# Six layers over sixteen images on one core: due values for each stage and layer in place of one for each stage

## The reference, cut to what matters

```python
x = L0(x, ctx, mask)   # cross attention with masked context, output projection, residual, layer norm
x = L1(x, ctx, ctx)    # cross attention, projection, residual, layer norm
# L2 has three parts:
x = x + causal_self_attention(ln1(x)) @ m_proj_w + m_proj_b     # "SELF"
x = x + cross_attention(ln2(x), ctx) @ c_proj_w + c_proj_b      # "CROSS"
x = x + relu(ln3(x) @ f_w1 + f_b1) @ f_w2 + f_b2                # "FFN", hidden width 1024
x = L3(x, ctx)         # layer norm, cross attention with weights rounded to {-1, 0, 1} * mean|W|
```

## Time and profile before

| | |
|---|---|
| median of 3 runs | 1466.26 us (1465.84 to 1468.56) |
| the profiled execution | 1464.82 us |
| its span, first to last instruction | 1463.1 us |
| instructions | 42292 |
| busy share: PE, DVE, ACT, POOL | 96%, 69%, 54%, 33% |
| mean granted TensorE clock | 0.991 |

### The profile page before, as it was taken

How to read it: one execution, slowest core, us unless ns; L and a number is a source line. 1 busy time by engine, 2 the same in 40 slices (tenths; PEclk the granted TensorE clock), 3 DMA queues, 4 the chain that set the end, 5 groups by cost and what they waited for, 6 DMA issues and landing times.

```text
span 1463.1 us, 42292 instructions
## 1 busy us (share of the span) xinstructions
PE 1404.4 (96%) x18408; PEld 1138.3 (78%) x18408; DVE 1005.1 (69%) x1895; ACT 783.9 (54%) x1305; POOL 481.4 (33%) x511
## 2 busy tenths in 40 slices
PE   4999999999999999999999999999989999899998
PEld 3777777777777777777777777778989999677775
DVE  3667677698787776666666677778686666656664
ACT  2565655655656555555555666665423334565663
POOL 6122213344444453332332221112485555000100
PEclk8999999999999999999999999999999999999999
DMA  7101000100000000000000100000000000000000
GB/s 290 37 26 43 23 26 15 52 9 16 9 9 9 31 16 2 2 2 2 2 2 16 45 9 9 15 9 23 30 1 1 2 1 8 16 30 30 30 24 30
DMA packets 14000, 34.79 MB, mean 24 GB/s; under 512 B 2167, under 2 KB 7543, under 8 KB 12407
## 3 DMA queue, kind: packets, MB, share of 16 engines
q1 hardware_dynamic: 13815, 32.09, 6.7%
HBM read 27.89 MB, written 4.19 MB: 22 GB/s over the span
## 4 chain that ended last, share of the span: by engine, by line
PE 82%; DVE 8%; ACT 5%; issue 2%; DMA 1%; POOL 1%; SPq 0%; DVEq 0%; ACTq 0%; POOLq 0%
PE ps L549 10%; PE ps L718 9%; PE ps L655 7%; PE ps L682 7%; PE ps L600 6%; PE ps L731 5%; PE ps L699 5%; PE ps L572 5%; PE ps L744 5%; PE ps L560 5%; ACT s_PU L841 4%; DVE s_nm L966 4%; PE ps L660 2%; PE ps L679 2%; PE ps L539 2%
## 5 line engine op out<-in xcount | busy, mean ns | idle before, releaser
L966 DVE TENSOR_REDUCE s_nm<-ps 128x8 fp32r<-128x960 f32 (+1 forms) x352 | 395.2, 1168 | 132.8 <-PE ps L600 74.8
L841 ACT ACTIVATE s_PU<-ps 120x1024 f32<-120x1024 f32 (+1 forms) x288 | 273.1, 1028 | 161.2 <-PE ps L660 161.2
L1105 POOL TENSOR_TENSOR s_xs<-s_xs,s_rowv 128x512 f32<-128x512 f32 x96 | 126.4, 1317 | 508.8 <-DVE s_nt L909 460.9
L655 PE MATMUL ps<-s_Qs,s_KH 32*120 32x256 f32 (+2 forms) x4608 | 180.3, 286 | 5.9 <-DVE s_xs L987 2.8
L655 PEld LDWEIGHTS ps<-s_Qs,s_KH 32*120 32x120 f32 (+1 forms) x4608 | 150.3, 181 | 41.2 <-issue 31.2
L549 PE MATMUL ps<-s_xT,s_W 128*128 128x256 f32 x640 | 163.4, 399 | 10.6 <-DMA s_xT<-x_t 9.4
L850 ACT ACTIVATE s_Os<-ps 128x512 f32<-128x512 f32 x160 | 94.4, 596 | 128.5 <-PE ps L682 83.4
L718 PE MATMUL ps<-s_W,s_oT 128*128 128x256 f32 x640 | 156.6, 387 | 1.3 <-ACT s_oT L857 0.9
L794 ACT ACTIVATE s_Qs<-ps,s_colv 128x256 fp32r<-128x256 f32 x160 | 67.2, 472 | 148.5 <-PE ps L549 148.5
L549 PEld LDWEIGHTS ps<-s_xT,s_W 128*128 128x128 f32 x640 | 118.2, 195 | 35.9 <-issue 11.1
L682 PE MATMUL ps<-s_PU,s_Vp 120*32 120x256 f32 x2048 | 126.3, 383 | 6.8 <-DVE s_nm L966 5.5
(11 more groups left out here) (89 smaller groups left out, 2334.6 us busy)
## 6 DMA issues: line engine op xcount, KB each, us to landing
s_cT<-ctx_t SPq DMA_DIRECT2D x32, 240.0 KB, 2.6
s_W<-w_att SPq DMA_DIRECT2D x5, 1024.0 KB, 5.0
s_xs<-x_nat SPq DMA_DIRECT2D x4, 1024.0 KB, 11.8
s_xT<-x_t SPq DMA_DIRECT2D x16, 256.0 KB, 2.7
out<-s_xs SPq DMA_DIRECT2D x16, 256.0 KB, 2.0
s_rowv<-rows SPq DMA_DIRECT2D x6, 512.0 KB, 4.2
s_W<-w_ff SPq DMA_DIRECT2D x2, 1024.0 KB, 5.1
s_mi<-mask SPq DMA_DIRECT2D x8, 120.0 KB, 3.7
```

The lines of the kernel that those rows point to most:

```text
L655: e.matmul(banks[j][0:n, wide * x:wide * x + wide], kz[row[j], lk, g, c, k0:k0 + n], q[row[j], lq, g, qs_], start=(x == 0 and y_ == 0), st ...
L841: t = e.activation(P_of(i, k)[0:n, :, :], pair("B", i, k)[0:n, :, :], ACT.Exp, scale=0.25)
L966: e.tensor_reduce(o, v, AX.X, ALU.max, negate=True).then_inc(sem["max"])
L1105: e.tensor_tensor(xs[:, b, :, :], xs[:, b, :, :], row2(layer, 0), ALU.add).then_inc(sem["pool"])
```

## The change

Only tables change. `WANT` has, for 40 of its names, six numbers in place of one, in the order L0, L1, SELF, CROSS, FFN, L3 (0 where the layer has no such stage), and a new function `want_of` picks the number of the image's layer. Other names keep a single number, mostly a new one. `STAY` goes from 0.121 to 0.656. The stages, their instructions, durations, buffers and the due values of the loads are the same.

```diff
-WANT = dict(xT=-3, cT=-4, mi=-4, bo=-0.9, N=0.88, T=-0.79, Te=-1.18, Q=0.15, Qh=3.01, Ql=-0.26, K=-0.32, Kh=1.79, Kl=0.17,
-            K0=1.54, V=0.81, Ve=3.52, mf=-1.83, A=0.45, max=0.53, M=0.88, mTe=1.15, B=1.08, exp=1.59, cap=2.76, PV=1.76,
-            PVe=2.77, ON=2.29, ONe=2.21, OT=3.16, OTe=1.33, O=-0.25, y=4.16, st=4.05, rs=2.36, ln=0.56, lng=3.08, X=1.12,
-            F1=-0.17, Fa=-0.09, Fv=-1.71, Hl=0.99, F2=2.13, out=2.2)
+WANT = dict(xT=-3, cT=-4, mi=-4, bo=(-1.68, 0.22, -6.66, -2.81, 8.53, -0.8), N=(0, 0, 8.9, 13.27, 16, 15.87),
+            T=(0, 0.35, -0.56, -0.63, -0.63, -1.54), Te=(0, -3.63, 7.25, 0.39, 3.9, 7.52), Q=(-0.03, 1.04, -0.05, 0.2, 0, -0.7),
+            Qh=(13.71, 9.56, 5.71, 14.01, 0, 16.38), Ql=(-5.91, -7.59, -4.02, -3.87, 0, -7.07), K=(-1.2, 0.19, -3.8, -0.22, 0, -1.34),
+            Kh=(0.13, 5.69, 7.44, 5.39, 0, -2.16), Kl=(-9.03, -2.25, -7.99, -2.54, 0, -7.35), K0=(6.12, -3.8, 6.11, 2.79, 0, 1.29),
+            V=(0.6, 1.21, 0.77, 0.78, 0, -0.35), Ve=(-3.25, -1.77, 5.04, -0.25, 0, 4.19), mf=6.27,
+            A=(0.16, -1.21, 0.14, 0.02, 0, -0.86), max=(-9.77, -14.1, -7.88, -12.94, 0, -11.23),
+            M=(0.31, -8.05, -4.85, 0.36, 0, -1.53), mTe=(-6.15, -3.46, -3.6, -9.69, 0, -3.43),
+            B=(-6.16, -2.85, -0.3, -4.22, 0, -10.75), exp=(-0.4, -10.96, -0.91, 1.95, 0, -1.93), cap=1.26,
+            PV=(1.46, 1.9, 1.57, 1.17, 0, 0.19), PVe=(2.71, 5.48, -3.59, 2.5, 0, -0.28), ON=(2.9, 2.81, 2.52, 2.61, 0, 1.54),
+            ONe=(-10.27, -9.28, 2.38, 8.64, 0, 0.42), OT=(3.84, 3.53, 2.9, 2.9, 0, 2.25), OTe=(7.7, -0.97, 1.81, 1.61, 0, 7.1),
+            O=(-5.23, -3.69, -7.13, 1.73, 0, -4.18), y=(2.66, 8.06, 11.95, 7.69, 11.03, 11.69), st=(8.72, 11.45, 4, 14.55, 4.4, 0),
+            rs=(-2.61, -1.4, 4.45, -4.43, 5.15, 0), ln=(12.59, 9.16, 0, 0, 0, 0), lng=(-11.98, 3.44, 0, 0, 0, 0), X=2.67, F1=-4.25,
+            Fa=5.14, Fv=-3.24, Hl=3.63, F2=1.25, out=2.2)
...
-STAY = 0.121
+STAY = 0.656
...
+def want_of(name, i):
+
+    v = WANT[name]
+    return v[LAYERS.index(layer_of(i))] if isinstance(v, tuple) else v
...
-        self.stages[key] = Stage(engine, key, at + (WANT[name] if want is None else want), LONG[name] if long is None else long,
+        self.stages[key] = Stage(engine, key, at + (want_of(name, i) if want is None else want), LONG[name] if long is None else long,
```

## The result

The changed kernel takes 1442.33 us (median of 4 runs, 1440.32 to 1444.05) against 1466.05 us for the kernel before on the same chip (median of 4). The ratio is 0.9836, with a 95% interval of 0.9817 to 0.9855: 23.7 us, 1.6%, faster. The forecast was 1453, the range 1437 to 1474. The profiled execution took 1442.51 us, 22.3 us less than that of before.

What follows compares the result with a forecast made beforehand. PE was taken as the bound, busy 1404.4 of 1463.1 us. Terms 4.5 + 2.5 + 2 + 1.5 + 2.5 = 13.0 us took the profiled 1464.8 to 1451.8; with the median 1.4 higher, forecast 1453, range 1437 to 1474.

Steps and rivals of the forecast that it cites:

- L3's start: First L3 images: K comes early, so F1 and F2 cover the attention chain's holes and half clock; 4.5 of 6.0 us won.
- the FFN's start: Where the FFN begins: DVE reaches qs sooner, shrinking waits of qm and F1 and half-clock time; 2.5 of 6.0 us won.
- the signs named beforehand: If right: no half clock at L3's beginning, F2 behind qm 2.9 us, about 500 turns, PE busy some 5 us less.
- the term for the other queues: SP, POOL and DVE: moved stages and loads are covered because POOL and DVE are idle often enough; taken at nothing.
- ON behind exp: PE's 50 waits of ON, about 0.19 us each, for an exp on ACT: 2 of 9.5 us won.
- PV behind max: In L0, three PV wait 1.27 us each for a max, which moves ahead on DVE: 1.5 of 3.8 us won.
- Turns: PE's array mode changes, 530 at about 0.09 us: 28 fewer, mostly in L0, win 2.5 us.
- The start: First loads and 9 to 56 us: load waits stay, only the filling stages change; nothing, bounds 4 us either way.
- The end: The last image's chain, with nothing left to reorder; no gain taken.
- The slower rival: Tight order exposes max and exp, slower on chip than tabled: 0.39 us per attention image, 31 us, 1484; chance 0.21.

Runs made afterwards that it cites:

- The run with K early: Changed kernel with K of images 80 and 81 due at 74 in place of 78.66: 1453.34 us, 11.0 us slower than the changed kernel.
- The narrow qw: Changed kernel with the three POOL instructions of each qw on 8 columns in place of 512: 1434.44 us.
- shortening the two: Each max over half its keys, each exp but those of eight images over half its columns: changed kernel 1415.77 us, kernel before 1430.04 us.
- STAY alone: Kernel before with its old table and only STAY raised from 0.121 to 0.656: 1502.49 us, ratio 1.0253.
- values alone: Changed kernel's new table with the old STAY of 0.121: 1502.64 us, ratio 1.0252 to the kernel before.
- L3's values alone: Kernel before with new values for layer L3 only and the old STAY of 0.121: 1472.75 us, ratio 1.0054.
- PE's values alone: New values for PE's stages and the new STAY; ACT, DVE and POOL keep the values of the kernel before: 1434.87 us, ratio 0.9792.
- the same, qs later: PE's values alone, with each of the four qs held back until the F2 of one FFN image (69 to 72) is done: 1435.08 us.
- PE's values and L3: PE's values alone, plus the new values of ACT, DVE and POOL for layer L3: 1435.04 us.

## Why the prediction was right, and where it was not

**The bound and the sign** held: PE at 96% before and after, the same instructions, the gain in what PE spends beside its bare 1305.2 us. The size was low, 13.0 us forecast against 22.3 (profiled) and 23.7 (medians), and the terms were wrong in most places. That the time still fell into the range is in part luck: the terms for L3's start and the FFN's start, 7.0 of the 13.0 us, won nothing, and places that had small terms or none won more than forecast. Of the signs named beforehand, the half clock at L3's start stayed and PE's busy time fell by 14.5 us and not by 5; at the FFN's start the F2 behind qm is at full clock, as foretold, but two stretches at half clock stand behind waits of F1 instead.

**L3's start**, 4.5 us forecast: the holes and the half clock stayed as they were. The step that failed was "K(80) can take one of the two KH buffers before the last FFN halves have theirs". K was due earlier, at 78.66, but F1 of image 79, due at 74.75, had its X in time: the X value of 81.67 is a rank on DVE, not a time, and DVE had room. So F1 took the buffer first, as before. The run with K early shows that the cover works, some 4 us, but that the order which comes with it costs more behind it: 11 us in all. (The stretch up to Q of image 84 is 2.8 us shorter; 1.6 of that is less work in it, the rest lies behind the hole.)

**The FFN's start**, 2.5 us forecast: qs did come sooner and the 1.93 us wait of qm is gone, but F1's waits for Fv grew from 2.2 to 6.7 us, and PE's time in FFN stages from 200.6 to 205.1; with the qm stages it is 204.0 and 205.8, a loss of 1.8 where 2.5 was to be won. The steps that failed are "so qs is reached sooner", which counted the gain of qs and not what qa and qw then meet, and the term for the other queues, "Taken at nothing": it weighed DVE and POOL by their shares of busy time, each by itself. The narrow qw shows 7.9 us that hang on the two engines meeting.

**ON behind exp and PV behind max**, 2 + 1.5 us forecast: ON's waits for the exp of the earlier trace rows fell by 5.1 us and PV's are gone (5.5 in the whole span before). But the ON term is not a gain by itself: T and K wait for exp in its place, and PE's waits for exp are 1.0 us more in all. What fell are the waits for max, by 8.8 us. In L0 and L1 left-over time fell from 15.4 to 7.9 and from 7.1 to 3.2 us in the stretches of the table. This is the term that was too small, and it is the middle of the layers, which I had called tight. That PE waits behind its readers of PSUM held: shortening the two took 9.4 us out of the distance. Which of the two would win was the wrong way round.

**Turns**, 2.5 us forecast for 28 fewer at 0.09: 39 fewer with the whole array at the end of SELF's A, at a measured 0.108 each 4.2 us; 23 fewer and 2.5 us in the other count. The mechanism held. What the term left out is that a turn costs less with a transpose behind it; the ledger, which counts that in, has 6.1 us for turns, 3.9 of them at the entry to the whole array. No run tested that part by itself.

**The start**, taken at nothing: it ends 0.3 us later (A of image 1), and PE's two waits for first loads are 18.1 us where they were 19.0. That stays within the 4 us either way.

**The end**: "nothing left to reorder". The last stretch took 4.6 us less, 3.4 of it left-over time (6.3 to 2.9). That step had looked at the last chain alone, not at the two images before it.

**The slower rival** named a mechanism that exists, but its price was worked out from the wrong gap. The scheduler's table is low for max and exp in every order alike, and the difference between chip and scheduler's clock shows no growth with urgency:

| kernel | scheduler's clock | chip, median | chip - clock |
|---|---|---|---|
| before | 1407.3 | 1466.1 | 58.7 |
| changed | 1389.3 | 1442.3 | 53.0 |
| STAY alone | 1442.3 | 1502.5 | 60.2 |
| values alone | 1448.1 | 1502.6 | 54.5 |
| L3's values alone | 1418.2 | 1472.8 | 54.6 |
| K(80) early | 1401.5 | 1453.3 | 51.8 |
| PE's values alone | 1390.6 | 1434.9 | 44.3 |
| the same, qs later | 1387.6 | 1435.1 | 47.5 |
| PE's values and L3 | 1390.6 | 1435.0 | 44.4 |

The clock spans 60 us from best to worst, the offset 16. The three lowest offsets are the three kernels that keep the old values for DVE, ACT and POOL (the last of them outside L3). 2 us of it lie at the FFN's start, with the collision that the scheduler does not know; the other part, 4 us in CROSS and SELF and 1 in L0, was not traced.

## What to carry to other kernels

Where lists are made by a greedy scheduler, a table of priorities is one point and not a sum of edits: two halves of this change cost 37 us each alone. Price it by the whole schedule (here the scheduler's own clock told the chip's time within some 8 us of a constant, good enough to refuse the bad orders but not to choose among good ones: it put PE's values alone 1.3 us behind the changed kernel, and the chip had them 7.5 ahead), and expect an earlier due value to do nothing where another stage with a still earlier one wants the same buffer. When PE is 96% busy, look for the rest in which stage stands behind a turn of the array and behind a reader of PSUM, in the middle of the layers, where a few tenths of a microsecond repeat 80 times; and try to give back the part of a change that touches engines off the bound, which here was worth 7.5 us more.

## What the runs showed of the hardware

A turn of the array costs 0.108 us, measured with 80 added round trips. By the timelines a round trip is paid in three places: 0.095 us by the last whole-array stage, about 0.1 by the last stage in rows, and 0.055 (before a transpose) to 0.10 (before a 256-column projection) by the first whole-array stage.

Some DVE instructions that read and write SBUF alone are held up by a POOL instruction that started before them, until it ends. A tensor_scalar of 512 columns took 0.55 us alone and 2.27 beside POOL's Hl; N, two instructions of 256 columns, takes 0.73 us alone and 2.35 beside Hl in the FFN. Others are not: BATCH_NORM_STATS2 from SBUF (L1014) took 0.41 us alone, and 0.41 (at most 0.43) in the 56 cases in which POOL was busy beside it. DVE's max and Fv, which read PSUM, kept their 1.16 and 0.48 us throughout (at most 1.23 and 0.49). The Trainium skill, in SBUF — State Buffer, section SBUF: two separate sides, has this as an exclusive lock: the port pair that DVE and GpSimd share goes to whichever starts first, for the whole instruction, if DVE's is in a two-port mode, or has two SBUF inputs and GpSimd's reads SBUF. The traces agree for L1035, which has two SBUF inputs, beside L1175, which reads SBUF. L1077 and N have one wide SBUF input; by that rule they would have to be in a two-port mode, which no trace here shows.

The granted clock fell to its lower level of 1.2 GHz behind the waits of 1.79 and 2.38 us at the FFN's start of the changed kernel, and F1 then took 4.63 and 4.62 us; behind the wait of 1.61 us it did not, and F1 took 3.14. At L3's start it fell in both kernels around three waits of 0.68, 0.69 and 1.2 us.
